# A gated linear-attention block in float32 on one core: tables loaded as rows, rows of statistics on another queue, five raw buffers, another order of splits

## The reference, cut to what matters

```python
hs = einsum('bct,bcd->bdt', x, cond_w[subjects])         # 64x64 matrix per sequence
q, k, v = hs @ Wq, hs @ Wk, hs @ Wv                      # 512 -> 16 heads x 128
beta = sigmoid(hs @ Wb + bb); gate = silu(hs @ Wg)
q = silu(causal_dwconv(q, qconv_w, qconv_b)); k = silu(causal_dwconv(k, kconv_w, kconv_b))   # 4 taps
q = layernorm(q.reshape(.., 16, 128), qn_w, qn_b); k = layernorm(.., kn_w, kn_b)
S = (1 - b) * S + b * outer(v_t, k_t); o_t = S @ q_t     # per head, over 64 steps
x = x + (o * gate) @ Wo
h = x' @ W2.T + adapter(x', A2[idx], B2[idx]) * scale    # rank 16, one of 8 adapters
gamma = mean(|ffn_w|, -1); w = clip(round(ffn_w / gamma), -1, 1)
x = x + (quantize(rmsnorm(h)) @ w.T) * gamma * x_scale + ffn_b
```

## Time and profile before

| | us |
|---|---|
| median of three runs | 2634.05 |
| the profiled execution | 2636.07 |
| its span in the trace | 2634.3 |

### The profile page before, as it was taken

One profiled execution on the slowest core, in us unless ns is written; L12 is line 12 of the kernel. 1 busy time (PEld: TensorE's weight loads), 2 busy tenths in 40 slices (PEclk: granted clock), 3 DMA queues, 4 the chain that ended last, 5 costly groups with the idle time before them and its releaser, 6 DMA issues. The chain is left out here.

```text
span 2634.3 us, 38353 instructions
## 1 busy us (share of the span) xinstructions
PE 2468.4 (94%) x14280; PEld 1859.6 (71%) x14280; DVE 1610.8 (61%) x2648; ACT 1075.1 (41%) x1615; POOL 781.0 (30%) x636
## 2 busy tenths in 40 slices
PE   5777888999999999999999999999999999999976
PEld 4555666777777777777777777777777777777754
DVE  2544445667666756667566765667656675667653
ACT  3444433444344534444444434444434433444321
POOL 2345433222222222232233222332322232233221
PEclk8888889999999999999999999999999999999987
DMA  6667566657666676666757576666766577666650
GB/s 170 236 220 244 198 225 220 224 177 244 228 205 200 199 235 223 218 204 205 257 186 232 194 246 201 226 196 201 264 200 222 171 234 236 193 214 210 228 170 16
DMA packets 339298, 551.38 MB, mean 209 GB/s; under 512 B 110762, under 2 KB 135338, under 8 KB 339114
## 3 DMA queue, kind: packets, MB, share of 16 engines
q1 hardware_dynamic: 339114, 548.93, 63.3%
HBM read 495.08 MB, written 53.74 MB: 208 GB/s over the span
## 5 line engine op out<-in xcount | busy, mean ns | idle before, releaser
L519 POOL TENSOR_TENSOR og_lo<-gt,og_hi 128x512 fp32r<-128x512 f32 x128 | 179.1, 1399 | 1124.6 <-ACT og_hi L990 1124.6
L1043 PE MATMUL pj_b<-ht_hi,wk 128*128 128x512 f32 x1024 | 358.6, 412 | 44.5 <-POOL wk L509 34.9
L1043 PE MATMUL pj_a<-ht_hi,wq 128*128 128x512 f32 x1024 | 361.3, 414 | 24.7 <-ACT gt L983 11.1
L1043 PE MATMUL pj_a<-ht_hi,wg 128*128 128x512 f32 x1024 | 354.6, 407 | 15.3 <-DMA wg<-parts_g 9.8
L794 DVE SCALAR_TENSOR_TENSOR y_q<-pj_a,conv,y_q 128x504 f32<-128x504 f32 (+2 forms) x384 | 281.1, 732 | 134.7 <-ACT y_q L966 125.4
L1043 PE MATMUL ring<-wo,og_hi 128*128 128x512 f32 x1024 | 325.5, 399 | 5.2 <-issue 5.2
L1043 PE MATMUL ring<-wv,ht_hi 128*128 128x512 f32 x1024 | 321.0, 395 | 9.1 <-POOL wv L509 9.1
L794 DVE SCALAR_TENSOR_TENSOR y_k<-pj_b,conv,y_k 128x504 f32<-128x504 f32 (+2 forms) x384 | 281.5, 733 | 74.3 <-ACT y_k L966 64.8
L515 POOL TENSOR_TENSOR y_k<-y_k,sq_k 128x512 f32<-128x512 f32 x128 | 170.3, 1331 | 502.7 <-DMA sq_k<-m_rows 502.7
L1043 PEld LDWEIGHTS pj_b<-ht_hi,wk 128*128 128x128 f32 x1024 | 199.1, 194 | 148.4 <-issue 52.0
L1043 PEld LDWEIGHTS pj_a<-ht_hi,wq 128*128 128x128 f32 x1024 | 197.9, 193 | 74.0 <-issue 13.4
(11 more groups left out here) (179 smaller groups left out, 4630.1 us busy)
## 6 DMA issues: line engine op xcount, KB each, us to landing
wq<-parts_q SPq DMA_DIRECT2D x112, 512.0 KB, 4.1
wk<-parts_k SPq DMA_DIRECT2D x112, 512.0 KB, 6.3
wg<-parts_g SPq DMA_DIRECT2D x112, 512.0 KB, 6.1
wv<-parts_v SPq DMA_DIRECT2D x112, 512.0 KB, 6.6
wo<-parts_o SPq DMA_DIRECT2D x112, 512.0 KB, 6.7
sq_q<-m_rows SPq DMA_DIRECT2D x128, 256.0 KB, 3.6
sq_k<-m_rows SPq DMA_DIRECT2D x128, 256.0 KB, 4.5
sq_q<-r_rows SPq DMA_DIRECT2D x128, 256.0 KB, 3.7
```

Of the source, the lines that this page charges most:

```text
L519: G.tensor_tensor(og_lo[:, u % OG_RING, :], gt[:, u % GT_RING, :], og_hi[:, u % OG_RING, :].bitcast(F32), ALU.subtract).then_inc(S["oglo"], 1)
L1043: last = T.matmul(psum, a, b, start=start and n == 0 and m == 0, stop=stop and n == len(pairs) - 1 and m == 2)
```

## The change

- **Tables as rows.** The convolution tables and norm weights are loaded with one row per head (2 KB and 512 B rows) on ScalarE's queue into `gt`; TensorE turns them with eleven small transposes into the `stat` bank, VectorE copies them to `conv` and `ln`. Four of the eight first conditioning loads move to ScalarE, with a semaphore for each pair. The two steps on Wb go behind `cond_lo`. B2 is one load, put in order by VectorE; gamma is turned by TensorE (tile `gr`, unit 4) and stored as four rows.
- **Rows of statistics.** For U < 20 (`ROWS_SP`) ScalarE issues the write and the four spreads itself; afterwards SyncE does, as before.
- **Raw buffers.** Five instead of four; raw blocks are loaded two ahead of the block that is saved (`RAW_LEAD`).
- **Order of splits.** q, k, then v or o, then g. On ScalarE v and o come behind the gate, q and k ahead of it; on GpSimd q is between the two affines, k ahead of the centring, v, o and g behind it.
- **SyncE.** In units 16 to 18 raw loads and saves come behind the loads of q and k, ahead of the keep rows and the load of g.

```diff
-RAW_SLOTS = 4
+RAW_SLOTS = 5
+RAW_LEAD = 2
+    ROWS_SP = H + 4
-            return own[:1] + SPLIT_PARTS.get(U, []) + own[1:]
+            return own[:2] + SPLIT_PARTS.get(U, []) + own[2:]
...
+            def split_traffic(U):
+                blocks = split_blocks(U)
+                for b in blocks:
+                    load_raws(split_no[b] + RAW_LEAD + 1)
+                    save_splits(split_no[b] - SAVE_LAG + 1)
...
+                if U in (H - 1, H + 2):
+                    save_splits(split_no[blocks[-1]] + 1)
...
+                if U < H:
+                    split_traffic(U)
                 if H <= U + 1 < UNITS:
                     load_head("q", U + 1)
-                if U % 2 == 0 and 2 <= U <= UNITS:
+                if U % 2 == 0 and ROWS_SP <= U <= UNITS:
                     send_means(U // 2 - 1)
                 if H <= U + 1 < UNITS:
                     load_head("k", U + 1)
-                if U % 2 and 3 <= U <= UNITS + 1:
+                if U % 2 and ROWS_SP <= U <= UNITS + 1:
                     send_rstd((U - 3) // 2)
+                if H <= U < H + 3:
+                    split_traffic(U)
...
@@ GpSimd
                     affine(U - 4)
+                for b in blocks:
+                    if b[0] == "q":
+                        split_lo(b)
+                if U % 2 == 0 and 4 <= U <= UNITS + 2:
                     affine(U - 3)
                 for b in blocks:
-                    if b[0] in "qvo":
+                    if b[0] == "k":
                         split_lo(b)
                 if U % 2 == 0 and 2 <= U <= UNITS:
                     centre_k(U - 2)
                     centre_k(U - 1)
                 for b in blocks:
-                    if b[0] in "kg":
+                    if b[0] in "vog":
                         split_lo(b)
@@ ScalarE, start
+            for i, (cw, cb) in enumerate(((qconv_w, qconv_b), (kconv_w, kconv_b))):
+                act.dma_start(conv_rows[:, i, :], cw.rearrange("(h p) t -> h (p t)", p=P)).then_inc(S["tab_in"], 16)
+                act.dma_start(small_rows[:, i * P:(i + 1) * P], cb.rearrange("(h p) -> h p", p=P)).then_inc(S["tab_in"], 16)
+            for i, w in enumerate((qn_w, qn_b, kn_w, kn_b)):
+                act.dma_start(small_rows[i:i + 1, 2 * P:3 * P], w.rearrange("(o p) -> o p", o=1)).then_inc(S["tab_in"], 16)
+            act.dma_start(bb_col[:], bb.rearrange("(p o) -> p o", o=1)).then_inc(S["tab_in"], 16)
+            act.wait_ge(S["subj_in"], 16)
+            act.wait_ge(S["setup_pool"], 2)
+            for b in range(ROWS // 2, ROWS):
+                subj = act.value_load(subj_row[0:1, bass.ds(b, 1)], min_val=0, max_val=cond_w.shape[0] - 1)
+                at = L * (b % 2)
+                act.dma_start(cond_pair[at:at + L, b // 2, at:at + L], cond_w[subj]).then_inc(S[f"c_first{b // 2}"], 16)
@@ ScalarE, a unit
                     keep_means(U // 2 - 1)
-                if U < UNITS:
-                    first_tap("k", U)
-                if U % 2 and 3 <= U <= UNITS + 1:
-                    seed((U - 3) // 2)
+                    if U < ROWS_SP:
+                        send_means(U // 2 - 1)
                 for b in blocks:
                     if b[0] == "q":
                         split_hi(b)
                 if U < UNITS:
+                    first_tap("k", U)
+                if U % 2 == 0 and 2 <= U < ROWS_SP:
+                    spread_means(U // 2 - 1)
+                if U % 2 and 3 <= U <= UNITS + 1:
+                    seed((U - 3) // 2)
+                if U < UNITS:
                     silu("q", U)
                     silu("k", U)
+                if U % 2 and 3 <= U < ROWS_SP:
+                    send_rstd((U - 3) // 2)
                 take(U, 0)
-                for b in blocks:
-                    if b[0] in "vo":
-                        split_hi(b)
                 for b in blocks:
                     if b[0] == "k":
                         split_hi(b)
+                if U % 2 and 3 <= U < ROWS_SP:
+                    spread_rstd((U - 3) // 2)
                 if U < UNITS:
                     gate(U)
                 for b in blocks:
-                    if b[0] == "g":
+                    if b[0] in "vog":
                         split_hi(b)
@@ TensorE, start
+            pe.wait_ge(S["tab_in"], 16 * TAB_LOADS)
+            pe.wait_ge(S["setup_pool"], 5)
+            for i in range(2):
+                for k in range(5):
...
+                    T.transpose(stat[:, (5 * i + k) * H:(5 * i + k + 1) * H], rows, ident[0:H, 0:H])
+            T.transpose(stat[:, 10 * H:10 * H + 4], small_rows[0:4, 2 * P:3 * P], ident[0:4, 0:4]).then_inc(S["turned"], 1)
             for t in range(HT):
                 make_cond(0, t)
```

More of the change, by code:

```diff
@@ L142, in adaln_attn_ffn @@
         hb = sb("hb", [P, 2, D])
-        raw = [rows_b[:, 0, :], rows_b[:, 1, :], hb[:, 0, :], hb[:, 1, :]]
+        raw = [rows_b[:, 0, :], rows_b[:, 1, :], hb[:, 0, :], hb[:, 1, :], sb("raw", [P, D])[:]]
         beta_row = xq[0:H].rearrange("p a d -> p (a d)").bitcast(F32)
@@ L284, in save_splits, with load_raws @@
                     saved[0] += 1
[L286 to L292, removed]
+            loaded = [0]
+            def load_raws(end):
+                while loaded[0] < min(end, len(split_order)):
+                    no = loaded[0]
+                    if no >= RAW_SLOTS:
+                        sp.wait_ge(S["w_split"], no - RAW_SLOTS + 1)
+                    sp.dma_start(raw_slot(split_order[no][0], no), block_src(*split_order[no])
+                                 ).then_inc(S[f"raw_in{no % RAW_SLOTS}"], 16)
+                    loaded[0] += 1
             def load_x(g):
@@ L381, in _ @@
             load_x(0)
-            load_raw(split_order[0])
-            load_raw(split_order[1])
+            load_raws(2)
             sp.wait_ge(S["subj_in"], 16)
             sp.wait_ge(S["setup_pool"], 2)
[L386 to L389, removed]
+            for b in range(ROWS // 2):
+                subj = sp.value_load(subj_row[0:1, bass.ds(b, 1)], min_val=0, max_val=cond_w.shape[0] - 1)
+                at = L * (b % 2)
+                sp.dma_start(cond_pair[at:at + L, b // 2, at:at + L], cond_w[subj]).then_inc(S[f"c_first{b // 2}"], 16)
             sp.dma_start(wb_raw, Wb.rearrange("(k p) h -> p k h", p=P)).then_inc(S["wb_in"], 16)
[L391 to L395, removed]
+            load_raws(3)
             def save_out(g, t):
@@ L609, in split_setup @@
                     hi, lo = (w[:].rearrange("p k c -> p (k c)") for w in (a_hi, a_lo))
[L610 to L613 removed]
+                src = bank_[:]
+                if kind == "sb":
+                    hi, lo = (w[:].rearrange("q (p j) -> q j p", j=KC) for w in (b_hi, b_lo))
+                    src = src.rearrange("q (j p) -> q j p", j=KC)
+                late_step(V.tensor_copy(hi, src))
+                V.tensor_tensor(lo, src, hi.bitcast(F32), ALU.subtract).then_inc(taken_sem(kind, 0, t), 1)
             def ternary():
@@ L959, in keep_means, with send_means, spread_means, send_rstd @@
                 A.activation(rstd[:], stat[:], ACT.Identity).then_inc(S["mean_kept"], 1)
+            def send_means(m):
+                act.wait_ge(S["mean_kept"], m + 1)
+                for j in range(4 if m else 0):
+                    act.wait_ge(S[f"m_in_{'qk'[j % 2]}{j // 2}"], 16 * m)
+                act.dma_start(m_rows, rstd[0:P:32, :]).then_inc(S["m_out"], 16)
+            def spread_means(m):
+                act.wait_ge(S["m_out"], 16 * (m + 1))
+                for j in range(4):
+                    x_ = "qk"[j % 2]
+                    if m:
+                        act.wait_ge(S[f"n_{x_}"], 2 * m - 1 + j // 2)
+                    act.dma_start(sq[x_][:, j // 2, :], m_rows[j:j + 1, :].broadcast_to([P, GROUP])
+                                  ).then_inc(S[f"m_in_{x_}{j // 2}"], 16)
+            def send_rstd(m):
+                act.wait_ge(S["rr"], m + 1)
+                for j in range(4 if m else 0):
+                    act.wait_ge(S[f"r_in_{'qk'[j % 2]}{j // 2}"], 16 * m)
+                act.dma_start(r_rows, rstd[0:P:32, :]).then_inc(S["r_out"], 16)
+            def spread_rstd(m):
+                act.wait_ge(S["r_out"], 16 * (m + 1))
+                for j in range(4):
+                    x_ = "qk"[j % 2]
+                    act.dma_start(sq[x_][:, j // 2, :], r_rows[j:j + 1, :].broadcast_to([P, GROUP])
+                                  ).then_inc(S[f"r_in_{x_}{j // 2}"], 16)
             def first_tap(x_, u):
```

101 lines of the change are left out of this document (58 added, 43 removed), and 2 rows, old and new, of the table FIRST_TILES.

## The result

| | before | after |
|---|---|---|
| median, us | 2634.91 (4 runs, 2629.78 to 2638.0) | 2574.07 (4 runs, 2570.72 to 2577.99) |
| the profiled execution | 2636.07 | 2573.15 |
| its span | 2634.3 | 2571.4 |
| first q projection at | 26.5 | 17.9 |
| units 0 to 19 | 447.6 | 392.5 |

The ratio is 0.977, with a 95% interval of 0.9753 to 0.9787: 60.8 us faster. The forecast was 2556, so the sign and the mechanism held and 18 us of the gain are missing. Against the profiled execution, for which the prediction gave 2558, the miss is 15 us; the other 3 are scatter between executions.

What follows compares the result with a forecast made beforehand. Bound by TensorE's idle time and low clock in units 0 to 19 (132 us), plus the start. Gains of 9 (start) + 68.6 (group) = 77.6 us give 2556 against the median, 2558 against the profiled execution; range 2528 to 2598.

Steps and rivals of the forecast that it cites:

- What bounds: Only the start and units 0 to 19 are open; there 132 us are lost, 89 idle and 43 to lower clock.
- The start: Ahead of the first q projection: tables on ScalarE's queue and shared conditioning loads bring it 9 us earlier, bounds 6 to 11.
- The group: Units 0 to 19, first 16 heads and seam: 447.6 us become 379, a gain of 68.6, bounds 30 to 95.
- the landing "2.5 later": First group: each row of means or rstd sent by ScalarE lands 2.5 us after its send, ahead of four spreads.
- the rival with late rows: First group: rows land after 6.7 us on average, each wait 4.2 longer, 50 us go back: 2606; 8 in 100.
- Unit 4: First group: unit 4 stays at 19 us, as the wait of 5.2 for GpSimd's affine stays.
- the light pair: Even then odd unit with only projections, bound by ScalarE's chain: 11.7 + 16.9 = 28.6 us; 32 with some lower clock.
- wk and gamma: First group: the row move gives the 34.9 us of waits on wk's half and the 12.3 before a score, behind gamma's store.
- The seam and unit 14: Waits: v in unit 14, 4.6 us; q at the seam behind wq's load, 6 to 7; wg in units 16 to 19, 3.5.
- the point of being wrong: Prediction wrong if ScalarE's waits for the rows sum to over 60 us, or the seam costs over 15.
- The rival of issue time: First group: moving rows saves only SyncE's issue time, 10 us over nine pairs; 2615 with the start's 9; 5 in 100.
- What would show it: Signs in start and group: q at 17 to 18 us, prompt sends, 2.5 landings, light odd units near 17, clock above 0.93.

Runs made afterwards that it cites:

- the doubled writes: The kernel after, with ScalarE writing each row of statistics to DRAM twice in the first group, the second behind the landed first: 2595.41 us, ratio 0.9847.
- the seam is mended: wq and wk of the next group loaded ahead of wo's saves: old order 2560.58 us; kernel after, also wg ahead of the saves of units 16 to 18, 2562.07 us.
- rows back on SyncE: The kernel after with rows of statistics back on SyncE behind its raw loads and saves, and splits in the order of the kernel before: 2616.94 us, ratio 0.9944.
- rows first on SyncE: The kernel after with rows of statistics on SyncE, issued ahead of the unit's raw loads and saves, new order of splits kept: 2613.61 us, ratio 0.993.
- old order: The kernel after with the order of splits of the kernel before, rows of statistics still on ScalarE: 2564.60 us, ratio 0.9748.

## Why the prediction was right, and what it missed

**What bounds.** Right. The stages named as open are the only ones that moved, and the work in them stayed 315 us.

**The start.** Right: 17.9 against 17 to 18, a gain of 8.6 where 9 was counted. Nine small loads took 0.23 to 1.05 us each on ScalarE's queue, 0.45 on average where 0.5 was estimated; the tables landed at 9.8, not 8.5, and the conditioning matmuls ran from 11.1 to 16.4. What was not counted: TensorE now goes from the conditioning into q with 1.5 us between and keeps full clock (unit 0: 14.1 us at 0.97, before 18.0 at 0.78). That is 4 us for nothing; it hides in the 66.2 for units 0 to 3, forecast as 66, since unit 1 fell to a clock of 0.73 and waited 2.5 for VectorE's taps.

**The group.** By stage, forecast and measured (us):

| units | before | forecast | after |
|---|---|---|---|
| 0 to 3 | 70.8 | 66 | 66.2 |
| 4 to 7 | 98.2 | 70 | 76.0 |
| 8 to 13 | 135.1 | 109.5 | 114.6 |
| 14, 15 | 59.1 | 56.5 | 57.3 |
| 16 to 19 | 84.4 | 77 | 78.4 |
| sum | 447.6 | 379 | 392.5 |

11 of the 13.5 us that are missing lie in units 4 to 13. The term that was mis-sized is the landing "2.5 later", taken for every row from one row of the trace. From the write to the first spread it measures 4.1 us on average for the means and 3.0 for rstd (up to 5.9), and the spreads behind it take 5.1 to 6.2 instead of 3.6 to 4.4. The trace of before already said so: there the nine rows of means took 2.5 to 7.7 us, 4.2 on average, and the row is the shortest of them. So for the means nothing got slower by the change; the figure was read from the best row. For rstd the time was 2.3 on average without the row behind gamma, and is 3.0 now. The direction was named as the rival with late rows (6.7 us, 2606); the times measured lie about a quarter of the way to that rival's. The range took it in. By the doubled writes they account for an estimated 9 to 11 us of the whole miss; gate waits of 21.3 us and the clock that falls behind them are the form it takes.

Two other terms were off in the same units. Unit 4, below, took 2.3 us more than forecast. And the even unit of the light pair (unit 8) was priced at 11.7 us by ScalarE's chain, while it holds 14 us of TensorE work (14.41 us busy at full clock before, 15.8 at 0.89 after): 2.4 us that no landing explains. The pair took 15.8 + 20.6 = 36.4 us where 32 was counted. How these terms and the landings share the 11 us is not settled.

**wk and gamma.** Both right: no wait of the k projection on wk is left, and the 12.3 before a score is gone. One transfer in pieces cost 9.2 us, shown alone.

**Unit 4.** Right in kind: GpSimd's affine is still late (6.6, was 5.2), the unit took 21.3, forecast 19 (19.7 before).

**The seam and unit 14.** Right in place and nearly in size: 5.5 for wq (6 to 7 forecast), 3.4 for wg (3.5), 4.5 for wv (4.6). But the one for wv is not a new wait, as the prediction has it: the 9.1 of the earlier trace rows stood at the same place of unit 14, behind raw blocks that came late, and the change halves it. The prediction priced these costs and did not draw the conclusion that the order of the loads at that place is a mistake, worth 12 us when mended (14 by the ratios), still under the 15 that I had set as the point of being wrong.

**The new order of splits.** I costed it as part of the whole and never alone. The runs show no gain from it: without it 2564.6, with it 2574.1 (the intervals overlap), and equal once the seam is mended. A term of its own in the sum would have shown that its gain is the last 12 us of waits on wk, against a gate held behind longer landings.

**The rival of issue time.** It fell: by it the rows would have given 10 us, they gave 52. In the Trainium skill, "DMA: Bandwidth & Descriptors", section "Issuing engines are not separate DMA queues" says that several issuers share the same 16 engines and save only issue time. The first half agrees with the runs here: a row issued by ScalarE landed in 1.7 us with nothing of SyncE's just ahead of it and in 2.9 to 4.6 with a save there. For the second the measurement decides otherwise: with SyncE 2616.9, with ScalarE 2564.6, since an issuer that waits in order holds all that is queued behind it.

**What would show it.** Sends within 1 us of the kept row: 88.76 after 88.73 in unit 4, and the same 0.03 in every pair. Landing 2.5 us later: missed, as above. Light odd units near 17: 17.2 for unit 5, but 20.6 for unit 9, whose row landed in 3.9. Granted clock above 0.93: missed, 0.92. ScalarE's waits attributed to issues and landings ahead of silu and gate: 47 us, under the 60 that I had set as the point of being wrong.

## What to carry to other kernels

A write that the same queue must wait for belongs on a queue in which nothing due stands behind the wait; moving it forward in a busy queue only changes who waits. Take the landing of a small write from many rows of the trace and not from one (here 2.5 was read where the nine rows had 4.2 on average), and ask which transfer goes out just ahead of it. When a group of blocks is reordered, follow each queue to the seam with the next loop: the loads that the other loop needs first must not stand behind the last stores of this one.

## What the runs showed of the hardware

- The same spread of 256 KB landed 3.4 to 4.8 us after its issue from SyncE's queue (before, rows back on SyncE, rows first on SyncE) and 5.0 to 6.4 from ScalarE's (after, old order), in medians, with the DMA share at 0.66 there and 0.74 to 0.76 here. Whether the queue or its company makes it slower was not tried.
- An 8 KB write from ScalarE's queue landed in 1.7 us in all nine pairs of the old order with no save of SyncE's in the 2.5 us ahead; in the kernel after it took 2.9 to 4.6 with a save there and 5.9 behind three loads of 512 KB. From SyncE's own queue it took up to 7.7, the one behind gamma apart (before).
- A store of 2 KB in 4-byte pieces held the 8 KB write behind it for 6.4 us.
- The DMA share reached 0.99 at 331 GB/s between 50 and 75 us in the kernel after, as before; it did not stall TensorE there, which was busy 23.5 of the 25 us.
